# State-space stage of a five-layer convolution and attention chain: whole-length scan, tanh in place of Silu, B and C split by TensorE

## What is computed

```python
xn = layer_norm(x)
xi, z = split(xn @ W_in.T)
xc = silu(conv4(xi) + conv_b)              # causal, 4 taps
dt, B, C = split(xc @ W_x.T, [4, 20])
delta = softplus(dt @ W_dt.T + b_dt)
h[t, d, n] = h[t-1, d, n] * exp(delta[t, d] * A[d, n]) + delta[t, d] * xc[t, d] * B[t, n]
y[t, d] = sum_n h[t, d, n] * C[t, n] + xc[t, d] * Dp[d]
out = (y * silu(z)) @ W_out.T + x
```

## Time and profile before

| | us |
|---|---|
| median of 3 runs (3407.79 to 3416.77) | 3412.4 |
| the profiled execution | 3417.81 |
| its span, first to last instruction | 3416.1 |
| PE busy | 3027.8 (89%) |
| DVE busy | 2520.3 (74%) |
| POOL busy | 2138.2 (63%) |
| ACT busy | 2043.1 (60%) |

### The profile page before, as it was taken

How to read it: one execution, slowest core, us unless ns; L and a number is a source line. 1 busy time by engine, 2 the same in 40 slices (tenths; PEclk the granted TensorE clock), 3 DMA queues, 4 the chain that set the end, 5 groups by cost and what they waited for, 6 DMA issues and landing times. The chain is left out here.

```text
span 3416.1 us, 54728 instructions
## 1 busy us (share of the span) xinstructions
PE 3027.8 (89%) x17582; PEld 1162.8 (34%) x17582; DVE 2520.3 (74%) x3283; ACT 2043.1 (60%) x2444; POOL 2138.2 (63%) x854
## 2 busy tenths in 40 slices
PE   5999999999999999999989997747887888788887
PEld 2334334334333333333323332512322222223222
DVE  4888888888788888888722221338888888889888
ACT  3577777777777777777653332335554556455654
POOL 0588888888888888888750000026666666666665
PEclk7899999999999999999999998869999999999999
DMA  4477777787777777777751210144343434344343
GB/s 131 117 180 169 187 183 177 181 186 171 177 181 177 177 182 179 178 182 182 185 156 68 74 43 35 64 153 141 118 161 118 147 130 146 132 131 147 130 149 117
DMA packets 112140, 498.88 MB, mean 146 GB/s; under 512 B 18489, under 2 KB 19325, under 8 KB 79565
## 3 DMA queue, kind: packets, MB, share of 16 engines
q0 software_dynamic: 31824, 214.97, 29.9%
q1 hardware_dynamic: 80092, 281.00, 23.6%
HBM read 192.29 MB, written 39.39 MB: 68 GB/s over the span
## 5 line engine op out<-in xcount | busy, mean ns | idle before, releaser
L673 DVE TENSOR_REDUCE at_pmax<-at_ring 128x1 f32<-128x512 f32 x2048 | 1292.5, 684 | 266.1 <-PE at_ring L443 256.9
L632 ACT ACTIVATE at_probs<-at_sc 128x1024 f32<-128x1024 f32 x1024 | 992.6, 1021 | 378.7 <-PE at_sc L526 378.4
L736 POOL TENSOR_TENSOR at_prob_sums<-at_prob_sums,at_probs 128x2048 f32<-128x2048 f32 x189 | 925.8, 4899 | 3.4 <-ACT at_probs L632 3.2
L1744 POOL TENSOR_TENSOR ss_drive<-ss_du,ss_bsb 128x1024 f32<-128x1024 f32 x261 | 611.1, 2354 | 270.4 <-DVE ss_state L1701 262.8
L519 PE MATMUL at_sc<-at_QT,at_KT 32*128 32x512 f32 x4096 | 738.5, 638 | 4.4 <-issue 4.0
L1644 ACT ACTIVATE ss_decay<-ss_delta,k_a 128x512 f32<-128x512 f32 x520 | 354.5, 687 | 446.9 <-DVE ss_state L1697 300.9
L538 PE MATMUL at_O<-at_probs,at_V 128*32 128x512 f32 x4096 | 528.2, 605 | 0.2 <-ACT at_probs L632 0.2
L1533 PE MATMUL ss_Y<-ss_seen,k_ident 128*128 128x512 f32 x1032 | 523.8, 632 | 0.0
L443 PE MATMUL at_ring<-at_KH,at_QH 32*128 32x512 bf16 x2048 | 457.4, 388 | 16.4 <-ACT at_KT L590 8.9
L1709 DVE TENSOR_TENSOR ss_seen<-ss_state,ss_C 128x1024 f32<-128x1024 f32 x259 | 316.1, 1221 | 87.4 <-PE ss_C L1521 79.6
L1701 DVE TENSOR_TENSOR_SCAN ss_state<-ss_decay,ss_state,ss_drive 128x512 f32<-128x512 f32 x259 | 332.2, 1282 | 31.4
(11 more groups left out here) (198 smaller groups left out, 2914.3 us busy)
## 6 DMA issues: line engine op xcount, KB each, us to landing
ss_bsb<-scratch_rows SPq DMA_DIRECT2D x265, 512.0 KB, 6.8
at_odd_sums<-at_probs POOLq DMA_DIRECT2D x126, 1024.0 KB, 7.9
at_odd_sums<-at_probs SPq DMA_DIRECT2D x63, 1024.0 KB, 5.0
at_prob_sums<-at_odd_sums POOLq DMA_DIRECT2D x63, 1024.0 KB, 7.5
scratch_attn<-at_att SPq DMA_DIRECT2D x64, 256.0 KB, 2.4
ss_xn<-scratch_xm SPq DMA_DIRECT2D x34, 256.0 KB, 5.5
at_xn<-scratch_xn SPq DMA_DIRECT2D x32, 256.0 KB, 6.2
k_att<-scratch_attn SPq DMA_DIRECT2D x16, 512.0 KB, 5.3
```

What stands on the lines that cost most here:

```text
L632: nc.scalar.activation(probs[:, kb, two, :].rearrange("p h q -> p (h q)"), sc[:, two, :].rearrange("p h q -> p (h q)"), ACT.Exp, scale=SCA ...
L673: nc.vector.tensor_reduce(pmax[:, quad // 2, h, quad % 2:quad % 2 + 1], ring[:, unit[3], :], AX_X, ALU.max, negate=True).then_inc(max_done, 1)
L736: nc.gpsimd.tensor_tensor(prob_sums[:, half, :, :], before, probs[:, POOL_ADDS[n], :, :], ALU.add).then_inc(pool_sums, 1)
L1744: nc.gpsimd.tensor_tensor(drive[:, n % DEPTH, :], du[:, par, :], bsb[:, n % SLOTS, :], ALU.mult).then_inc(drive_done, 1)
```

## The change

- **Scan.** `scan` is one instruction over 1024 positions, and `make_decay` one exp over 1024 positions, which waits for the whole scan of the step before.
- **Silu.** silu(v) is made as v/2 * (1 + tanh(v/2)). ACT makes v/2, tanh, and 1 + tanh (`take_x`, `bend_x`, `bend_z`, `take_z`), POOL the product (`make_u`, `make_gate`). The table set `exp_and_others` holds exp and tanh; the set with the logarithm is loaded behind `take_low` (step 11) and the other again in step 13.
- **Split of B and C.** ACT copies B and C in fp32 into `bc_all`. Units MID and LOW (steps 10 and 11) let PE form the remainder: identity times `bc_all` in fp32, minus the bf16 parts so far. ACT rounds each remainder to bf16 (`take_mid`, `take_low`). DVE's and POOL's subtractions are gone.
- **Side by side.** The two halves of the unit delta lie on different rows of the array (32 and 64), those of z on rows 0 to 63 and 64 to 127, those of the output product on different columns. `res` and `xw` are now 128 by 512.
- **Other moves.** The multiplication by the gate goes from DVE to POOL (`make_yv`), from a copy of Y that ACT takes (`take_y`). The residual is added by POOL (`add_xw`) and no longer by PE. The output product moves from step 1 to 2. LEAD is 3. The image's input is loaded an image ahead, in `between`. Units stand behind `add_state` in a step and no longer ahead of it. Set-up gets two more small weight loads and one more filler row block in DRAM.

```diff
+        for half in range(2):
+            sp.dma_start(self.w_in[half * C:(half + 1) * C, :], a["L3_conv_W_in"]).then_inc(self.ss, DMA)
...
+        for row in (2 * N, 4 * N):
+            sp.dma_start(self.w_dt[row:row + R, :], a["L3_conv_W_dt"]).then_inc(self.ss, DMA)
...
-        LEAD = DEPTH - 2
-        AT_X, AT_CONV, AT_Z, AT_BC, AT_REST, AT_MID, AT_DT, AT_LOW, AT_DELTA = 6, 6, 8, 9, 10, 11, 12, 12, 13
+        LEAD = DEPTH - 1
+        X0, X1, BC, DT, MID, LOW, Z = range(7)
+        UNIT_AT = {3: X0, 4: X1, 7: BC, 9: DT, 10: MID, 11: LOW, 12: Z}
+        UNITS = 6
...
+                sp.wait_ge(sum_done, b + 1)
+                for h in range(2):
+                    sp.dma_start(out_d[bass.ds(b, 1), :, hs(h)].rearrange("a c s -> (a c) s"), res[h * C:(h + 1) * C, :])\
+                        .then_inc(stored, DMA)
...
-                if n == TURN:
-                    sp.wait_ge(gate_done, b + 1)
-                    load_x(b + 1)
...
+                sp.wait_ge(z_done, 3 * b + 5)
+                load_x(b + 2)
                 store(b)
-                load(xw[:, 1 - par, :], xw_d, b + 1, xw_in)
...
+                load_xw(b + 1, 1 - par)
...
+                elif k == Z:
+                    pe.wait_ge(low_done, b + 1)
                     for h in range(2):
-                        for k in range(KC // 2):
-                            m = nc.tensor.matmul(aux[:, hs(h)], w_taps[:, k, :], xn[:, h * HALF + 2 * k:(h + 1) * HALF + 2 * k],
-                                                 start=(k == 0), stop=(k == KC // 2 - 1))
-                elif k == 1:
+                        at = KC - 1 - h + h * HALF
+                        m = nc.tensor.matmul(aux[:, hs(h)], w_in[h * C:(h + 1) * C, DI:2 * DI], xn[h * C:(h + 1) * C, at:at + HALF],
+                                             start=True, stop=True)
+                    m.then_inc(aux_ready, 1)
...
+                elif k == DT:
+                    pe.wait_ge(dt_done, 3 * b + 3)
...
                     for h in range(2):
+                        rows = slice(2 * N * (h + 1), 2 * N * (h + 1) + R)
                         m = nc.tensor.matmul(aux[:, hs(h)], w_dt[rows, :], dt[rows, hs(h)], start=True, stop=True)
...
+                elif k == MID:
+                    pe.wait_ge(abs_done, 2 * b + 1)
+                    pe.wait_ge(relu_done, b + 1)
+                    pe.sem_inc(split_open, 1)
+                    for h in range(2):
+                        nc.tensor.matmul(aux[0:2 * N, hs(h)], ident[0:2 * N, 0:2 * N], bc_all[:, par, hs(h)], start=True, stop=False)
+                        m = nc.tensor.matmul(aux[0:2 * N, hs(h)], minus[0:2 * N, :], bc[0:2 * N, par, hs(h)], start=False, stop=True)
+                    m.then_inc(aux_ready, 1)
+                elif k == LOW:
+                    pe.wait_ge(mid_done, b + 1)
+                    pe.sem_inc(split_open, 1)
+                    for h in range(2):
+                        nc.tensor.matmul(aux[0:2 * N, hs(h)], ident[0:2 * N, 0:2 * N], bc_all[:, par, hs(h)], start=True, stop=False)
+                        m = nc.tensor.matmul(aux[0:2 * N, hs(h)], minus[:], bc[0:4 * N, par, hs(h)], start=False, stop=True)
+                    m.then_inc(aux_ready, 1)
...
+                        units(*now)
...
+                        if now[2] == TURN - 1:
+                            pe.wait_ge(yv_done, b + 2)
...
                             for h in range(2):
-                                nc.tensor.matmul(aux[0:C, hs(h)], w_out[:], yv[:, hs(h)], start=True, stop=False)
-                                m = nc.tensor.matmul(aux[0:C, hs(h)], ident[0:C, 0:C], xw[:, g, hs(h)], start=False, stop=True)
+                                m = nc.tensor.matmul(aux[h * C:(h + 1) * C, hs(0)], w_out[:], yv[:, hs(h)], start=True, stop=True)
...
-                nc.scalar.activation(gate[:, par, :], aux[:], ACT.Silu).then_inc(gate_done, 1)
...
+                nc.scalar.activation(pre[:], aux[:], ACT.Identity, bias=half_bias[:], scale=0.5).then_inc(pre_done, 1)
...
+            def bend_x(b):
...
-                nc.scalar.activation(u_in[:, par, :], pre[:], ACT.Silu).then_inc(u_done, 1)
-                nc.scalar.preload_act_table_set("natural_log_exp_and_others")
+                nc.scalar.activation(tanh_x[:], pre[:], ACT.Tanh).then_inc(tanh_done, 1)
+                act.wait_ge(tanh_done, 2 * b + 1)
+                nc.scalar.activation(tanh_x[:], tanh_x[:], ACT.Identity, bias=1.0).then_inc(tanh_done, 1)
...
+            def bend_z(b):
...
+                nc.scalar.activation(tanh_z[:], aux[:], ACT.Tanh, scale=0.5).then_inc(z_done, 1)
+            def take_z(b, par):
+                nc.scalar.activation(gate[:, par, :], aux[:], ACT.Identity, scale=0.5).then_inc(z_done, 1)
+                act.wait_ge(z_done, 3 * b + 1)
+                nc.scalar.activation(tanh_z[:], tanh_z[:], ACT.Identity, bias=1.0).then_inc(z_done, 1)
...
+            def take_hi(b, par):
...
+                nc.scalar.activation(bc[0:2 * N, par, :], aux[0:2 * N, :], ACT.Copy).then_inc(dt_done, 1)
...
             def take_dt(b, par):
-                act.wait_ge(aux_ready, 4 * b + 3)
-                nc.scalar.activation(bc[0:2 * N, par, :], aux[0:2 * N, :], ACT.Copy).then_inc(hi_done, 1)
-                nc.scalar.activation(dt[2 * N:2 * N + R, :], aux[2 * N:2 * N + R, :], ACT.Copy).then_inc(dt_done, 1)
...
+                for h in range(2):
+                    to = 2 * N * (h + 1)
+                    nc.scalar.activation(dt[to:to + R, hs(h)], aux[2 * N:2 * N + R, hs(h)], ACT.Copy).then_inc(dt_done, 1)
...
+                nc.scalar.activation(bc_all[:, par, :], aux[0:2 * N, :], ACT.Copy).then_inc(brow_done, 1)
...
+            def soft_exp(b):
...
+                nc.scalar.activation(soft[0][:], soft[0][:], ACT.Exp, scale=-1.0).then_inc(abs_done, 1)
...
+            def take_mid(b, par):
...
+                nc.scalar.activation(bc[2 * N:4 * N, par, :], aux[0:2 * N, :], ACT.Copy).then_inc(mid_done, 1)
...
+            def take_low(b, par):
...
+                nc.scalar.activation(bc[4 * N:6 * N, par, :], aux[0:2 * N, :], ACT.Copy).then_inc(low_done, 1)
+                nc.scalar.preload_act_table_set("natural_log_exp_and_others")
...
+            def soft_log(b):
...
                 nc.scalar.activation(soft[1][:], soft[0][:], ACT.Ln, bias=1.0).then_inc(soft_done, 1)
...
+            def back_to_exp():
+                nc.scalar.preload_act_table_set("exp_and_others")
...
             def take_out(b):
...
+                nc.scalar.activation(res[:], aux[:, hs(0)], ACT.Copy).then_inc(res_done, 1)
...
+            def take_y(b):
+                act.wait_ge(y_ready, (b + 1) * N + DEPTH)
+                act.wait_ge(yv_done, b + 1)
+                nc.scalar.activation(y_out[:], Y[:], ACT.Copy).then_inc(y_step, 1)
...
-                for h in range(2):
...
+                if not (isinstance(b, int) and b == 0 and n == 0):
+                    act.wait_ge(state_done, b * N + n + DEPTH)
+                nc.scalar.activation(decay[:], delta[:, par, :], ACT.Exp, scale=a_neg[:, n:n + 1]).then_inc(decay_done, 1)
...
                 make_decay(*ahead(b, par, n, 1))
-                if n == 2 and not isinstance(b, int):
+                if n == 0 and not isinstance(b, int):
+                    take_y(b - 1)
+                if n == TURN - 1 and not isinstance(b, int):
                     take_out(b - 1)
-                if n == AT_X:
+                if n == 4:
                     take_x(b + 1)
-                if n == AT_Z:
...
-                if n == AT_BC:
...
+                    bend_x(b + 1)
+                if n == 7:
+                    take_hi(b + 1, 1 - par)
+                if n == 8:
                     take_dt(b + 1, 1 - par)
...
-                    take_b(b + 1, 1 - par)
...
-                    middles(b + 1, 1 - par)
...
-                    softplus(b + 1)
+                if n == 9:
+                    take_delta(b + 1)
+                if n == 10:
+                    soft_exp(b + 1)
+                    take_mid(b + 1, 1 - par)
+                if n == 11:
+                    take_low(b + 1, 1 - par)
+                if n == 12:
+                    soft_log(b + 1)
+                if n == 13:
+                    back_to_exp()
+                    bend_z(b + 1)
+                if n == 14:
+                    take_z(b + 1, 1 - par)
 
...
-                dve.wait_ge(hi_done, b + 1)
-                nc.vector.tensor_tensor(bc_rest[:], aux[0:2 * N, :], bc[0:2 * N, par, :], ALU.subtract).then_inc(rest_done, 1)
...
-                nc.vector.tensor_tensor_scan(now[:, hs(0)], decay[:, hs(0)], drive[:, n % DEPTH, hs(0)], 0.0,
-                                             ALU.mult, ALU.add).then_inc(first_half_done, 1)
...
-                nc.vector.tensor_tensor_scan(now[:, hs(1)], decay[:, hs(1)], drive[:, n % DEPTH, hs(1)], now[:, HALF - 1:HALF],
+                dve.wait_ge(decay_done, b * N + n + 1)
```

(33 more changed lines are left out.)

199 lines of the change are left out of this document (93 added, 106 removed).

## The result

| | before | changed |
|---|---|---|
| median | 3413.16 us (3407.79 to 3416.77) | 3278.73 us (3276.74 to 3284.26) |
| ratio | | 0.961, 95% interval 0.9592 to 0.9628 |
| profiled execution, its span | 3417.81, 3416.1 us | 3284.26, 3282.4 us |
| first scan to end of last | 1110.7 us | 957.0 us |
| per image, (last scan's start - first's) x 16/258 | 68.7 us | 59.2 us |

The account below looks back on a forecast made before the run. DVE bounds the last phase: 259 steps of 3.46 us, plus 3.2 of waits and 1.2 of clock for 16 images, give 966.5 against 1110.7; with +10 start-up and +3 at the end, net -131, 3281 us, range 3250 to 3345.

Parts of the forecast that it names:

- Scan and step: Last phase, DVE: one 1024-position scan takes 2.28 us, and a step 3.46, 0.33 less, with DVE and ACT tied.
- Stalls: Waits per image: 0.23 at decay 12, 2.67 at scan 13, 0.3 for `pre`; 3.2 us in place of 7.4.
- TensorE: PE work per step: half pairs 0.95 us each, MID and LOW 2.6 each, the 2.12 wait behind the output product gone.
- Clock: PE at half rate in the last phase: costs 1.2 us an image, between 0 and 3.5, where it cost 2.2 before.
- Ends: Outside the scan loop: +10 us ahead of the first scan, +3 behind the last.
- Silu by tanh: ACT's Silu replacement: gives nothing by itself, three more ACT passes all under scans, table loads still two an image.
- The drain: Rival at ACT's table loads: each takes 2.66 us, 2.5 an image, +40, 3321; chance 0.03.
- Units at the wrong time: Rival on PE: MID, LOW and delta run at 1.2 GHz, the wait at steps 12 and 13 grows, +75, 3356; chance 0.15.
- TensorE at half rate: Rival: PE becomes the bound at 1.2 GHz, kernel slower than before, +178 us at share 0.6, 3459; chance 0.04.
- The dearer scan: Rival on DVE: the 1024-position scan takes 2.43 us, +34, 3315; chance 0.10.
- pairs that don't overlap: Rival on PE: z, delta and output pairs cost 1.76 us, 1.6 an image, +26, 3307; chance 0.10.
- The long scan that buys nothing: Rival: decays exposed, each hand-over between scan and decay costs 0.15 more, step 3.8 us, +80, 3361; chance 0.04.

## Why the prediction was right

- **Scan and step.** 2.28 was forecast, 2.29 measured; the long one has the fixed share only once. That share, 0.15, was taken from a reduction and a product; no row before showed it for a scan, and that it fits (2 x 1.22 - 2.29 = 0.15) was partly luck. The step of 3.46 came out as 3.47 to 3.48 in 81 of the 227 steps without a wait, from scan 15 to scan 3 or 5 of an image, and as 3.54 to 3.55 in the other 146; with the waits of 2.43 and 0.44 taken off, 59.2 leaves 3.52 a step. This term was low by 0.06 x 259 = 16 us. The part of it that was mis-sized is the hand-over from the decay to the scan, 0.03 in ACT's sum. Two decays of the changed kernel, ahead of the scans at 2680.22 and 2712.45 above:

```profile
2679.07 1.12 ACT L1713 ACTIVATE ss_decay<-ss_delta,k_a 128x1024 f32<-128x1024 f32 x1 [2.36 <-DVE ss_state L1776]
...
2711.23 1.12 ACT L1713 ACTIVATE ss_decay<-ss_delta,k_a 128x1024 f32<-128x1024 f32 x1 [0.17 <-DVE ss_state L1776]
```

Both start with `seen` and take 1.12. The scan follows the first by 0.03 and the second by 0.10, and so it is in all steps of the longer kind (0.09 to 0.11); at scan 13, where DVE has long been idle, it is 0.10 too. So the step is 2.29 + 0.03 + 1.12 + 0.10 = 3.54. The tie of DVE and ACT, which I had seen and costed at nothing, is thus lost to ACT in two steps of three. With two half decays, which have slack, `seen` to scan is 1.14 in every step. Why the hand-over takes 0.10 in these steps isn't settled.
- **Stalls.** 0.23 + 2.67 + 0.3 = 3.2 forecast. Measured 2.43 at scan 13, 0.44 at scan 6 for `pre`, nothing at decay 12: 2.9, so this term was high by 0.3 x 16 = 5 us. Moving the load and then LOW took the first away in two steps, so its cause is shown: the load, and the units' place.
- **TensorE.** Pairs 1.13 and 1.08 (output), not 0.95: mis-sized, with cover. LOW 2.58 for 2.6, MID 2.26. The wait of 2.12 behind the old output product went, and came back with it (2.27).
- **Clock.** 1.2 an image was charged; the stage ran at a granted clock of 0.99, nearly all at 2.4 GHz, and each image took 59.2 to 59.3. This term was high by most of 19 us, and it hid the error in the step: 16 low, 5 and up to 19 high. The first scan to the end of the last took 957.0, 966.5 was forecast. The mechanism of the main terms held, the scan, the stall at scan 13 and the wait behind the output product; that the total came within 3 us is partly luck, since errors of opposite sign met, and the phases ahead took 5 us more.
- **Ends.** Start-up +10 forecast, from 38.7 to 49.8 it is +11.1; MID and LOW are 8.6 of it. From the end of the last scan to the end 11.1 us against 7.3: +3.8 for 3.
- **POOL.** 50.6 an image forecast, 50.9 in a window of 60 us is 50.2; inside the loop no scan waited for a drive. Costed at nothing, rightly, but POOL has little to spare: with the logarithm 1.3 us later it is `yv`, and not a drive, that is late first.
- **Silu by tanh** "gives nothing by itself": wrong as put. With Silu itself four loads are needed now that x and z are bent in different steps, and the image takes 1.6 more.
- **Rivals.** The drain is not seen: each load of 1.28 in the rows above has its next instruction 0.01 to 0.02 behind its end, where the two loads of step 5 stand one instruction apart too. The Trainium skill, in ScalarE: Activation LUTs, section What ACT_TABLE_LOAD costs, states it, some 1.38 us on top of the load and 2.66 a switch; the traces of this kernel don't agree. Units at the wrong time and TensorE at half rate (the slower case) fall too: MID and LOW take 2.26 and 2.58, and the clock is 0.99. The dearer scan and pairs that don't overlap fall by one row each. The long scan that buys nothing falls by the step, but its mechanism is there in part: 0.07 more at the hand-over, where it asked for 0.15 at each.

Where the 9.5 us an image came from, each part taken back by itself: scan 2.8, output product 2.8, separate rows 0.8, tanh 1.6, the split of B and C 0.0 (this one on the version with the moved load). The gate product off DVE wasn't tried by itself; its spacing was 1.14. Together 9.1; they need not add up, since a part taken back meets the slack of the others. The clock isn't in the list: its cost before was put at 2.2 an image, and it rose from 0.93 to 0.99 with the whole change. With the scan, the output product or the rows taken back it stays at 0.99, and the long scan alone, on the kernel before, brings it to 0.94. What it gave isn't separated.

## What to carry to other kernels

Give one engine's rhythm as the unit of account, and then ask of every helper how much it may do between two of its obligations: here ACT has 2.3 us behind each decay, and each wait for a decay was something over that. Count a change's enabling parts as parts: the earlier load of the input, two pieces of 256 KB, takes no work off any engine, and without it an image takes 14 us more, which is over twice what the scan and the output product bring together. It was not tried alone on the kernel before. Work moved off the bound engine is only won if it doesn't come back as a wait; for B and C 1.14 was taken off and 1.03 put in its place. And ask what a later instruction of a helper makes late behind it: the load moved by a step took 1.44 us off scan 13, and 0.6 came back in steps 4 and 5 of the next image, by way of POOL.

## What the runs showed of the hardware

- A scan over 1024 positions takes 2.29 us, over 512 from zero 1.22, over 512 from a carried state 1.28.
- A scan with decay and drive both in SBUF takes 2.29 us when it starts with POOL idle, and 3.13 to 4.4 beside a busy POOL, whose products take 4.34 instead of 2.35. With the decay in PSUM both keep their 2.29 and 2.35.
- Two fp32 half products on separate row blocks take 1.13 us, on the same rows 1.98.
- A hand-over from ACT to DVE takes 0.03 us in some steps and 0.10 in others, in blocks of several steps; for a scan of 2.29 that waits for nothing else this is the difference of 3.47 and 3.54. What decides isn't known.
- In the version with LOW moved, the granted clock fell from 1.00 to 0.59 behind ten microseconds in which PE was busy 9.76 and DMA at its full share. Before, it fell behind an idle gap of 2.59. Idle time ahead of it is thus not the only way there; what else decides is open. An image earlier the same stretch (2632 to 2642, PE busy 9.73, DMA share 0.99) was followed by a clock of 1.00.
